# Row maxima before the softmax: key differences computed once and stored, differences and scores on two halves of TensorE's rows, the first operand stacks loaded in the stage before

## The reference, cut to what matters

```python
x = L0_attn_x                                  # (4, 2048, 256)
xn = _layernorm(x, axis=-1)
qkv = xn @ Wqkv.T                              # 16 heads of width 16
dots = jnp.einsum('bhid,bhjd->bhij', q, k) * 16 ** -0.5
dots = jnp.where(causal_mask, -jnp.inf, dots)  # only keys j <= i
attn = jax.nn.softmax(dots, axis=-1)           # needs each row's maximum
out = jnp.einsum('bhij,bhjd->bhid', attn, v)
x = x + (out @ Wout.T + bout) + fp4_gated_layer(xn, w_gate, w_up, w_down)
```

## Time and profile before

| | |
|---|---|
| time, median of 3 runs | 2459.28 us (2459.23 to 2459.46) |
| the profiled execution's own time | 2462.13 us |
| its span | 2460.3 us |
| TensorE busy (matmuls) | 2295.5 us, 93% |
| VectorE busy | 2032.9 us, 83% |
| ScalarE busy | 1952.6 us, 79% |
| GpSimd busy | 666.0 us, 27% |
| weights and projection | 0 to 197.7 us |
| start of the maximum stage, no reduce yet | 197.7 to 220.4 us |
| maximum stage, first to last reduce | 220.4 to 928.3 us |
| attention with the gated layer | from there to 2460.3 us |

### The profile page before, as it was taken

The page is one execution under the profiler, slowest core; times in us unless marked ns, Lnnn a source line. Parts: engine busy times, 40 slices in busy tenths (PEclk is TensorE's granted clock), DMA queues, the critical chain, the costliest instruction groups (busy, mean ns, idle before and its releaser), DMA issues.

```text
span 2460.3 us, 85898 instructions
## 1 busy us (share of the span) xinstructions
PE 2295.5 (93%) x34104; PEld 1274.1 (52%) x34104; DVE 2032.9 (83%) x5926; ACT 1952.6 (79%) x3342; POOL 666.0 (27%) x530
## 2 busy tenths in 40 slices
PE   5995999999999998999999999999999999999998
PEld 4883444444444444555555555555555555555555
DVE  5977999999999997778877787777787777778776
ACT  2445999999999997888877788877788877878875
POOL 2324344244333422222222222221212212122221
PEclk8997999999999999999999999999999999999999
DMA  5665455444554461101201111111011022011000
GB/s 151 210 216 87 68 79 78 70 67 74 78 76 67 68 110 33 30 16 32 64 24 39 31 33 30 59 31 38 22 41 32 18 66 45 19 41 32 14 21 32
DMA packets 94544, 143.91 MB, mean 58 GB/s; under 512 B 24896, under 2 KB 73920, under 8 KB 93632
## 3 DMA queue, kind: packets, MB, share of 16 engines
q1 hardware_dynamic: 89792, 129.50, 26.2%
q0 software_dynamic: 4352, 8.92, 1.5%
HBM read 104.20 MB, written 34.14 MB: 56 GB/s over the span
## 4 chain that ended last, share of the span: by engine, by line
PE 47%; issue 6%; ACT 6%; DVE 3%; POOL 0%; DVEq 0%; ACTq 0%; POOLq 0%
PE O L1168 16%; PE F L1189 10%; PE S L1147 10%; ACT probs L1298 6%; PE F L1226 5%; PE F L1235 2%; PE F L1215 2%; PE S L1153 1%; DVE o_turned L1491 1%; DVE o_turned L1492 0%; PE S L1235 0%; PE F L1182 0%; DVE o_sum L1496 0%; DVE xt_lo L1441 0%; DVE o_packed L1503 0%
## 5 line engine op out<-in xcount | busy, mean ns | idle before, releaser
L1298 ACT ACTIVATE probs<-S 128x1024 f32<-128x1024 f32 (+3 forms) x1280 | 1077.3, 897 | 233.2 <-PE S L1153 129.6
L924 ACT ACTIVATE m_excess<-m_DIFF 128x512 f32<-128x512 f32 (+7 forms) x1536 | 647.4, 473 | 84.3 <-PE m_DIFF L884 39.0
L942 DVE CUSTOM_DVE_ANT_0 m_excess<-m_S,m_excess 128x512 f32<-128x512 f32 (+7 forms) x1536 | 700.7, 530 | 11.9 <-PE m_S L884 9.7
L1168 PE MATMUL O<-probs,v_sb 64*32 64x512 f32 (+3 forms) x10240 | 613.2, 532 | 1.0 <-ACT probs L1298 1.0
L882 PE MATMUL m_S<-m_k,m_q 128*128 128x512 f16 (+7 forms) x1536 | 482.7, 324 | 26.8 <-DVE m_row_max L942 17.4
L882 PE MATMUL m_DIFF<-m_k,m_q_diff 128*128 128x512 f16 (+7 forms) x1536 | 477.6, 318 | 25.7 <-DMA m_q_diff<-s_q 25.4
L1147 PE MATMUL S<-q_st,k_st 64*32 64x512 f16 (+3 forms) x10240 | 407.6, 350 | 61.2 <-ACT probs L1298 49.5
L1147 PEld LDWEIGHTS S<-q_st,k_st 64*32 64x32 f16 x10240 | 146.6, 90 | 391.2 <-ACT probs L1298 258.9
L835 POOL TENSOR_TENSOR m_q_diff<-m_zero,m_q 48x4096 f16<-48x4096 f16 x32 | 224.4, 7013 | 414.8 <-DMA m_q<-s_q 400.4
L1362 POOL TENSOR_TENSOR h_norm<-gated,h_rscale 128x704 f32<-128x704 f32 x64 | 89.0, 1391 | 806.2 <-DVE h_rscale L1415 806.2
L882 PEld LDWEIGHTS m_S<-m_k,m_q 128*128 128x128 f16 x1536 | 148.2, 96 | 276.2 <-DVE m_row_max L942 195.3
(11 more groups left out here) (190 smaller groups left out, 3901.8 us busy)
## 6 DMA issues: line engine op xcount, KB each, us to landing
m_q<-s_q SPq DMA_DIRECT2D x96, 128.0 KB, 3.7
m_k<-s_k SPq DMA_DIRECT2D x96, 128.0 KB, 6.6
m_q_diff<-s_q SPq DMA_DIRECT2D x96, 128.0 KB, 7.9
k_st<-s_k SPq DMA_DIRECT2D x96, 128.0 KB, 4.4
q_st<-s_q SPq DMA_DIRECT2D x384, 32.0 KB
m_k<-s_k SPq DMA_DIRECT2D x96, 124.0 KB, 5.1
a_x<-in_L_attn_x_dram POOLq DMA_DIRECT2D x16, 512.0 KB, 5.2
s_q<-a_part SPq DMA_DIRECT2D x32, 256.0 KB, 2.5
```

Of the source, the lines that this page charges most:

```text
L924: act.activation(excess[u % MAX_EXCESS][:, 0:keys // 2], DIFF[u % MAX_BUFS][:, 0:keys // 2], ACT.Relu) \
L942: dve.tensor_tensor_reduce(larger, S[u % MAX_BUFS][:, 0:keys // 2], larger, 1.0, -3e38, ALU.add, ALU.max, column).then_inc(reduced[u % MAX ...
L1168: ins = pe.matmul(O[e][s * SLOT:(s + 1) * SLOT, st.skip:QC], v_sb[st.group % 2][rows, st.j, s * SLOT:(s + 1) * SLOT], probs[s // 2][st.n % ...
L1298: act.activation(probs[half][st.n % PROBS][:, :, 0:st.width], S[half][:, :, 0:st.width], ACT.Exp, scale=scale).then_inc(exped[half], 1)
```

## The change

- **Key differences stored.** In the projection ScalarE copies each group's k (2 x 512 columns) from PSUM to SBUF once more (`a_k`). GpSimd subtracts each key from the one 64 after it and splits the result in two float16 parts (`key_differences`, three operations, one group behind). SyncE stores them (`s_kd`, two DMAs a group). TensorE's k products of the next group wait for ScalarE's copy (`k_copied`).
- **Two row halves.** A stack has 64 rows below for q and k and 64 rows above for q and the stored differences. Difference products use rows 64 to 127 and score products rows 0 to 63, all with all 128 columns of the array. The negation on GpSimd is gone. Masks are products over the same 64 rows.
- **Units of a whole query block.** 16 units a head of up to 1024 columns, in buffers of two banks, two for differences and two for scores; narrow blocks share a buffer, one in each bank. Excess buffers are six of 1024 columns. Differences run one unit ahead of scores (`MAX_LEAD` 1). The join is gone.
- **Early stacks.** The stacks lie in memory that the attention stage later uses for `o_heads` and `y` (`shared`). GpSimd clears half of it in the weights stage and half, with the masks, at the start of the projection; SyncE loads the first two stacks after groups 7 and 9 of the projection (12 DMAs each).

```diff
 # weights_phase, GpSimd
             gated_w.clear(pool)
+            pool.wait_ge(gated_w.cleared, 3)
+            stacks.clear(pool, 0)
...
 # projection_phase, GpSimd
             load_x(1, 0)
+            for p in range(2):
+                pool.wait_ge(rstd_ready[p], 1 + PRIMED)
+            stacks.clear(pool, 1)
+            stacks.masks(pool, ident)
+
+            def key_differences(r, p):
+                blocks = k_whole[p][:, :, :].rearrange("p o (n e k) -> p (o n) e k", e=2, k=PAIR)
+                before = later(r, p, -1)
+                pool.wait_ge(k_copied[p], r + 1 + PRIMED)
+                pool.wait_ge(diff_part1[before[1]], before[0] + 1 + PRIMED)
+                pool.tensor_tensor(k_diff[:, :, :].rearrange("p o (n k) -> p (o n) k", k=PAIR), blocks[:, :, 1, :],
+                                   blocks[:, :, 0, :], ALU.subtract).then_inc(k_differenced[p], 1)
+                pool.wait_ge(k_differenced[p], r + 1 + PRIMED)
+                pool.wait_ge(diff_st[p], r * (16 * PARTS) + PRIMED)
+                pool.tensor_copy(diff_part[0][p][:, :, :], k_diff[:, :, :]).then_inc(diff_part0[p], 1)
+                pool.wait_ge(diff_part0[p], r + 1 + PRIMED)
+                pool.tensor_tensor(diff_part[1][p][:, :, :], k_diff[:, :, :], diff_part[0][p][:, :, :], ALU.subtract) \
+                    .then_inc(diff_part1[p], 1)
...
 # body, GpSimd, after make_rstd and load_x
+                if g:
+                    key_differences(*later(r, p, -1))
...
 # TensorE
                     pe.wait_ge(part1_done[h][before[1]], before[0] + 1 + PRIMED)
+                    if h == 1:
+                        pe.wait_ge(k_copied[before[1]], before[0] + 1 + PRIMED)
...
 # ScalarE
                     turned_high(*later(r, p, 1))
+                act.wait_ge(part1_done[1][p], r + 1 + PRIMED)
+                act.wait_ge(k_differenced[p], r + PRIMED)
+                act.activation(k_whole[p][:, :, :], QK[:, 2:4, :], ACT.Copy).then_inc(k_copied[p], 1)
...
 # SyncE, after the store of v
+                if g:
+                    store_differences(*later(r, p, -1))
+                if g in FIRST_LOADS_IN:                      # (7, 9)
+                    for half in range(2):
+                        sp.wait_ge(parts_st[half], T // GRP // 2 * (16 * 2 * PARTS) + PRIMED)
+                        sp.wait_ge(diff_st[half], T // GRP // 2 * (16 * PARTS) + PRIMED)
+                    stacks.load(sp, 0, FIRST_LOADS_IN.index(g), dram)
...
-MAX_KEYS = 1024
-MAX_BUFS = 4
-MAX_EXCESS = 8
-MAX_LEAD = 2
+MAX_COLS = T // 2
+MAX_HALF = MAX_COLS // 2
+MAX_EXCESS = 6
+MAX_LEAD = 1
...
+    wide = [(i, NKB + NKB // 2 - 1 - i) for i in range(NKB - 1, NKB - NKB // 4 - 1, -1)]
+    narrow = [(i, NKB // 2 - 1 - i) for i in range(NKB // 2 - 1, NKB // 4 - 1, -1)]
+    for n, pair in enumerate(wide):
+        units += [MaxUnit(i, buf, 0) for buf, i in enumerate(pair)]
+        if n % 2 == 0:
+            units += [MaxUnit(i, buf, at) for buf in range(2) for at, i in zip((0, MAX_HALF), narrow[n + buf])]
...
+    def load(self, sp, b, load, dram):
+        p, head = load % 2, load * MAX_LOAD
+        sp.wait_ge(self.cleared, 4)
+        load_stack(sp, self.q[p], dram["q"], Q_STACK, head, MAX_LOAD, bass.ds(b * T, T), self.ld[p])
+        load_stack(sp, self.k[p], dram["k"], K_STACK, head, MAX_LOAD, bass.ds(b * T, T), self.ld[p])
+        load_stack(sp, self.q[p][ROWS:P, :, :], dram["q"], Q_STACK, head, MAX_LOAD, bass.ds(b * T, T), self.ld[p])
+        load_stack(sp, self.k[p][ROWS:P, :, 0:T // 2], dram["kd"], K_STACK, head, MAX_LOAD, bass.ds(b * T // 2, T // 2), self.ld[p])
...
 # TensorE, maximum stage: holders(n, u) is the last unit before u that used one of its banks
+            def difference(n, u, c0, c1):
+                h, unit = round_units[u]
+                pe.matmul(DIFF[unit.buf][:, unit.at + c0:unit.at + c1],
+                          q_st[h // MAX_LOAD % 2][PAIR:P, h % MAX_LOAD, unit.block * P:(unit.block + 1) * P],
+                          k_st[h // MAX_LOAD % 2][PAIR:P, h % MAX_LOAD, c0:c1], start=True, stop=c1 < unit.cols)
...
+                if lead:
+                    difference_ready(*lead)
+                    for cut in lead_cuts:
+                        difference(*lead, *cut)
+                    masks(DIFF, round_units[lead[1]][1], slice(PAIR, P), differed)
+                if at:
+                    pe.wait_ge(reduced, holders(*at) + PRIMED)
+                    for cut in cuts:
+                        score(*at, *cut)
+                    masks(S, round_units[at[1]][1], slice(0, PAIR), scored)
```

More of the change, by code:

```diff
@@ L418, in _ @@
             over_groups(body)
+            key_differences(*later(0, 0, groups - 1))
         @block.vector
@@ L581, in _ @@
                 sp.wait_ge(v_st[p], 16 * rounds + PRIMED)
+                sp.wait_ge(diff_st[p], 16 * PARTS * rounds + PRIMED)
 Q_STACK, K_STACK = (0, 1, 0), (0, 0, 1)
@@ L760, in load_first, with shift_phase @@
         self.load_tile(sp, 1)
-def shift_phase(nc, once, loop_sems, ident, dram, ahead, last_shift):
+def shift_phase(nc, once, loop_sems, dram, ahead, last_shift, stacks, ident):
     units = max_units()
-    assert len(units) % MAX_EXCESS == 0 and MAX_HEADS * NKB == P
-    split = MAX_KEYS // P
+    assert sorted(unit.block for unit in units) == list(range(NKB)) and MAX_HEADS * NKB == P
     primed = []
@@ L810, in loads_before, with before, holders @@
             return n * (loads // 2) + load // 2
-        round_units = [(h, *unit) for h in range(MAX_HEADS) for unit in units]
-        def uses(n, u, bufs):
-            return n * (len(round_units) // bufs) + u // bufs + 1
+        round_units = [(h, unit) for h in range(MAX_HEADS) for unit in units]
+        total = B * rounds * len(round_units)
+        def before(n, u):
+            return n * len(round_units) + u
+        def holders(n, u):
+            banks = set(round_units[u][1].banks)
+            for back in range(1, len(units)):
+                if before(n, u) >= back and banks & set(round_units[u - back][1].banks):
+                    return before(n, u) - back + 1
+            return 0
@@ L838, in store @@
-            def store(n, negates):
-                for p in range(2):
-                    pool.wait_ge(q_negated[p], negates + PRIMED)
+            pool.memset(last_shift.minus_unit[:, :], -1.0 / UNIT).then_inc(unit_made, 1)
+            pool.wait_ge(unit_made, 1)
+            ahead.fill(pool, ident)
+            for n in range(B * rounds - 1):
                 last_shift.split(pool, n)
@@ L889, in differences, with masks, difference_ready @@
+            def masks(out, unit, rows, done):
+                end = unit.at + unit.cols
+                pe.matmul(out[unit.buf][:, end - PAIR:end], masked[rows, :], future[rows, :],
+                          start=False, stop=True).then_inc(done, 1)
+            def difference_ready(n, u):
+                h, unit = round_units[u]
                 if u % per_load == 0:
                     load = h // MAX_LOAD
-                    pe.wait_ge(stack_ld[load % 2], loads_before(n, load) * (16 * load_dmas) + 16 * load_dmas + PRIMED)
@@ L904, in _ @@
-            pe.wait_ge(consts, 6)
-            for b in range(B):
-                for r in range(rounds):
-                    n = b * rounds + r
-                    for u in range(MAX_LEAD):
-                        differences(n, u)
-                    for u in range(len(round_units)):
-                        if u + MAX_LEAD < len(round_units):
-                            differences(n, u + MAX_LEAD)
-                        scores(n, u)
+                    pe.wait_ge(stacks.ld[load % 2], (loads_before(n, load) + 1) * (16 * stacks.dmas))
@@ L1605, in bass_attention_beside_fp4_gated_layer @@
             wts["down_" + half] = sb("w_down_" + half, [P, ITILES, D], F32R)
+        shared = [sb(f"shared{n}", [P, 2 * T]) for n in range(2)]
+        stacks = MaxStacks(sem, shared)
+        stacks.allocate(nc, ctx, sem)
         with ExitStack() as first:
```

238 lines of the change are left out of this document (111 added, 127 removed).

## The result

After: 2588.26 us (median of 4 runs, 2586.65 to 2589.65) against 2459.37 before on the same chip; ratio 1.052, 95% interval 1.050 to 1.054. The change made the kernel 129 us slower, where I had forecast 31, with 2512 as the range's upper end. The profiled execution took 2586.65 for a span of 2584.9, 124.6 more than before's span of 2460.3.

| part of the span | before | after | difference | my forecast |
|---|---|---|---|---|
| until the maximum stage's block opens | 197.7 | 213.7 | +16.0 | +1.5 |
| from there to the first reduce | 22.6 | 2.1 | -20.6 | -19.9 |
| first reduce to the last one's end | 707.9 | 837.5 | +129.6 | +51, less 1.8 |
| the rest | 1532.0 | 1531.6 | -0.4 | 0 |

What follows compares the result with a forecast made beforehand. VectorE was taken to bound the maximum stage, TensorE the projection. 51 - 19.9 + 0.5 + 1 - 0.3 - 1.5 = +31 on the 2459.3 median made 2490 us, range 2446 to 2512.

Steps and rivals of the forecast that it cites:

- the overlap is the 27 ns of a mask: Maximum stage, TensorE: in-order queue lets the row halves overlap only by a mask, 3 us off at most.
- rival A: Maximum stage: halves overlap, a waiting score doesn't hold the other half's differences back; 11.10 us a head, kernel 2448; chance 0.17.
- my 51: Maximum stage: VectorE's idle makes 11.78 us a head, 759 us with round changes, 51 us longer than before.
- Rival C: Maximum stage: TensorE at 1.2 GHz, 16.2 us a head for its columns, 280 us on top of the sum; chance 0.03.
- Neither is moved: Projection: GpSimd's three key operations, below 3.0 us of a 9.4 us group, delay neither reciprocal root nor x load.
- its cover lasts to 17.5: Start of the kernel: GpSimd's first memset pair ends at 10.8 us, within cover lasting to 17.5.
- I take 1 in all: Projection: early stack loads beside x loads may cost VectorE waits of 0 to 4 us each; 1 us taken in all.
- The 87% of VectorE: Maximum stage: VectorE busy 87% of the time, against 99.5% before.
- VectorE's price of a unit: Maximum stage: a unit holds VectorE for 1.04 ns a column plus 77 ns.
- before which units the idle would stand: Maximum stage: VectorE idles before 960, 832, 896, 768, 512 and 1024 columns, 1.50 us a head.
- the early start: Start of the maximum stage: with stacks and masks ready, first reduce at 200.5 instead of 220.4 us, 19.9 less.
- ScalarE's copy of the keys: Projection: the copy costs 1.02 us but has 3.0 us of cover before TensorE wants the bank.

Runs made afterwards that it cites:

- e2: The changed kernel with differences and their masks also on the lower 64 rows, so no products run side by side: 2845.1 us.
- e1: The changed kernel with every difference, score and mask multiplied over all 128 rows, same units, buffers and queue order: 2510.8 us.
- e4: The changed kernel with the earlier 24 units a head, four one-bank buffers per product and a lead of two: 2459.2 us, ratio to before 0.9995.
- e5: e4 with products on only the 48 data rows of each half and without the four memsets: 2456.7 us, ratio to before 0.9996.
- p2: The changed kernel without GpSimd's three operations on key differences, stored differences being zeros: 2583.0 us.
- p3: The changed kernel with the first two stack loads issued behind the projection's last stores of differences: 2595.6 us.
- e3: The changed kernel with each difference product issued twice, the second over the first: 2573.3 us.

## Why the prediction was wrong

The direction was right; the size was not, by 98 us. Step by step:

- **"TensorE takes its queue in order ... the overlap is the 27 ns of a mask."** The first half held, the second failed. A waiting score does hold the other half's difference back (269.45 and 269.46), so rival A's ground isn't there; but released products overlap by far more than a mask (both at 215.62). At the low clock that helped: 13.09 us a head against the 17.10 of e2, which has no overlap. e1, which takes all overlap away and is at full clock, lasts 50.8 us longer than before against my 51.
- **Rival C, the clock, "Unlikely", 0.03.** This is the step that failed and cost most: the sum prices every column at 0.417 ns, the upper level, and the stage ran at 0.53. Of the 78.5 us by which the stage passed my 759, at least 60 are the low clock's, by the change's own stretches at either level. I reasoned with how long TensorE streams (8.1 of 11.8 us a head) and not with how many rows; e1 against e2 shows that 64 rows in place of 128 take the level from 2.4 to 1.2 GHz at equal columns and order. At 1.2 GHz, 16.2 a head was my price for a serial queue; e2 has 17.10. The halves side by side made up for most of it: 13.09.
- **The two together** turn +51 into +129.6. Neither the units alone (e1, +50.8) nor the halves alone (e4, +1.6; e5 at 0.50 throughout, +3.9) add up to that: a low clock lengthens exactly the round trips that two buffers can't cover. What the change's whole stage would take at 2.4 GHz wasn't seen, since its stretches at that level caught half of the units. It is 12.2 us a head at most, where before had 11.06: whether units, buffers and halves would pay at the upper level stays open.
- **"Neither is moved"** (GpSimd's operations beside VectorE's), **"its cover lasts to 17.5"** (the memset) and **"I take 1 in all"** (the loads) failed: +16.0 where I had 1.5. I had looked at who waits for GpSimd by semaphore, and not at what runs beside it. What I took for the memset's cover was VectorE's w_spread, which takes 3.38 us beside it and 0.48 without; of the rest, p2 and p3 give the key operations' share and the loads'.
- **Busy share.** The 87% of VectorE was too low for its own sum: e1 has my 759 us with 695.1 busy, 92%, since the end of a reduce counts as busy where nothing follows at once.
- **Right:** VectorE's price of a unit (1225 ns at 1024 columns); before which units the idle would stand; the early start, 20.6 us for 19.9; ScalarE's copy of the keys, which no row shows TensorE waiting for; nothing changed behind the stage.

## What to carry to other kernels

Splitting TensorE's rows between two products doesn't double its pace if the granted clock halves; read the clock of the stretch first, and expect that the number of rows can change it, as it did here. Products of two halves overlapped here only once both were released; a queue that waits for one waits for both. Before making units larger at the price of buffers, work the round trip out at the lower clock too; if VectorE bounds the stage, buffers as deep as here (four a product) make TensorE's clock nearly a matter of indifference: 2.3 us between e4 and e5. Work that is moved to GpSimd beside a busy VectorE, and loads that are moved beside others, are priced by what runs beside them, not by who waits for them.

## What the hardware showed that I had not expected

- At equal columns and order, 128 rows ran at a granted clock of 1.00 (e1) and 64 at 0.50 (e2), with TensorE nearly without pause in the latter; with deep buffers 64 rows gave 0.77 (e4) and 48 rows 0.50 (e5).
- Matmuls of two row halves start within 10 ns of each other and out of program order (215.62 and 216.02 us). But a product that waits for a semaphore holds the other half's next one: a difference whose bank had been free since 268.41 started at 269.46, 7 ns after the waiting score.
- Both levels came in turns in one steady loop (e3: 0.50 from 221 to 271, 1.00 from 286 to 403), and a head took 16.7 and 12.4 us.
- A two-scalar operation of VectorE on 256 columns took 408 ns before, 706 on average beside GpSimd's memsets and key operations (674 without the memsets, 457 without the key operations); batch statistics of the same columns did not change (412 ns before, 408 after).
